# A fused attention and feed-forward kernel: the wide products of the layer stage cut into four products of 32 rows each

## Chip, cores and metric

The kernel runs on one core of a Trainium2 chip. The metric is the device time of one execution in microseconds (us); less is better.

## What is computed

The reference adds eight blocks to x, of 16 sequences x 256 tokens x 128 numbers, one after the other: a cross attention, a stack of six layers, and six further blocks. The change touches only the stack of six layers (`_L0_ffn_ref`). What matters of one layer, with 16 heads of 64 and windows of 32 tokens:

```python
qkv = shift_tokens(x) @ Wqkv              # 128 -> 3 * 1024
q, k = l2norm(q) * qs, l2norm(k) * ksc    # then rotated by position
sim = einsum('bhwie,bhwje->bhwij', q, look(k)) * 8.0      # each window looks at itself and the one before
x = x + einsum('bhwij,bhwje->bhwie', softmax(masked sim), look(v)) @ Wo
hg = layer_norm(shift_tokens(x)) @ W1 + b1                # 128 -> 2 * 341
a, gate = split(hg, 2)
x = x + (a * gelu(gate)) @ W2 + b2                        # 341 -> 128
```

All tensors are float32.

## The kernel before

The layer stage is `shifted_layers` (from L549). It works in 48 passes (`LAST`: 6 layers x 8 passes, p in the code) over 512 tokens, that is 4 tiles (t) of 128 tokens. A tile's heads go in two groups (g) of 8, so a pass has 8 such half tiles. Each engine has its own order of work, written out by hand, and the engines meet through semaphores only. TensorE's order is `body(p)` (L987 to L1140); it works on half tiles of several passes at once, so that other engines have time between two steps of one half tile.

What TensorE does in a pass, by the line of its instruction:

- `project_k` (L860) and `project_q` (L866), 8 times each: one product of the tile's 128 tokens (held in the array, 128 columns) with 512 columns of the weights, into the whole of a PSUM bank.
- `values_a`, `values_b` (L874), 16 times: four products, each with 32 tokens held and 512 columns streamed, each into 32 rows of one bank. The first two stream one slice of `w_vo`, the last two another.
- `scores` (L906) and `mix` (L930), 8 times each: 16 products of 32 held and 128 streamed columns, four for the four blocks of 32 rows and that for four blocks of columns.
- `turn_q` (L890), `turn_k` (L896), `turn_prob` (L917), 8 times each, and `turn_normed` (L952) once: four transposes of 128x128. `turn_x` (L845), twice: two such.
- `fold` (L943), once: one product of 256 columns.
- `gate_proj` (L962) and `up_proj` (L972), 3 times each: one product of 128, 128 and 85 held columns of `w_1` with 512 tokens. `down_proj` (L981), once: for each of 4 tiles three products that add up, 128 held and 128 streamed columns.

Every float32 product appears in the trace as two records, every transpose as one. Below, a group that holds 128 columns or 85 (a transpose, a fold, a product) is called wide, and one whose products hold 32 columns and write 32 rows is called narrow; before the change `values`, `scores` and `mix` are the narrow ones. The order of one steady pass is this, after its last step comes the first of the next pass. Square brackets mark the groups that are narrow before, round ones those that the change edits; 0, 1, 2 is the chunk k of gate and up.

```
turn_q (proj_k) (proj_q) turn_k up2 turn_prob [values_a] [scores] turn_q (proj_k) (proj_q) fold
turn_prob [values_b] [mix] turn_x (proj_k) turn_k [values_a] [mix] [scores] (down) (proj_q) turn_q
[values_b] (proj_k) turn_k turn_prob [values_a] turn_n (proj_q) turn_q [values_b] [scores] turn_k
(proj_k) (gate0) [values_a] [mix] [scores] turn_prob [values_b] turn_q (proj_q) (proj_k) turn_k
turn_prob (gate1) (proj_q) [mix] [values_a] [scores] turn_q turn_prob [values_b] turn_k gate2
(proj_k) (proj_q) [values_a] [scores] [mix] turn_x (proj_k) [mix] turn_q [values_b] (proj_q) turn_k
turn_prob (up0) [values_a] [scores] turn_q (up1) turn_prob [values_b] turn_k [mix] [values_a]
[scores] [mix] [values_b]
```

The other engines take their data from PSUM: ScalarE squares and copies, VectorE rotates, sums and finds the softmax's maxima, GpSimd adds and scales, and SyncE issues the transfers, weights of the next layer among them.

Of the kernel before, what the change touches and what calls it, by code (L numbers as in the profile page):

```python
# [24 lines left out]
DEPTH, WINDOW, HALF = 6, 32, 341  # L25
# [523 lines left out]
def shifted_layers(nc, x_all, ident, ident_bf, dram, kept, following):  # L549
# [17 lines left out]
    with ExitStack() as ctx:  # L567
        def sb(name, shape, dt=F32):
            return ctx.enter_context(nc.sbuf_tensor("f_" + name, shape, dt))
# [3 lines left out]
        def sem(name):  # L573
            used.append(ctx.enter_context(nc.semaphore("f_" + name)))
            return used[-1]

        bank = [ctx.enter_context(nc.psum_tensor(f"f_bank{i}", [128, 512], F32)) for i in range(8)]
        Q, K, V, T, S, P, Y, F = range(8)

        def flat(i):  # L580
            return bank[i][:, :]

        w_qk, w_vo, w_1, w_2, ln_cols, cols, rot, band, rot_dram = (
            kept[n] for n in ("w_qk", "w_vo", "w_1", "w_2", "ln_cols", "cols", "rot", "band", "rot_dram"))
# [20 lines left out]
        f_nt = sb("f_nt", [128, PASS_TOK])  # L605
        gate = sb("gate", [128, 3, PASS_TOK])
# [18 lines left out]
        q_done, k_done, q_squared, k_squared = sem("q_done"), sem("k_done"), sem("q_squared"), sem("k_squared")  # L625
# [10 lines left out]
        f_gate, gate_in, f_gelu, f_up = sem("f_gate"), sem("gate_in"), sem("f_gelu"), sem("f_up")  # L636
# [5 lines left out]
        def count(p, i):  # L642

            return p * CHUNKS + (i + 1 + AHEAD)

        def live(p, t):

            return not isinstance(p, int) or isinstance(p, Steady) or 0 <= p * PASS_TILES + t < LAST * PASS_TILES

        def has(p, back):  # L650

            return not isinstance(p, int) or isinstance(p, Steady) or 0 <= p - back < LAST
# [186 lines left out]
        def _(pe):  # L839
            nc.tensor.matmul(flat(S), ident_bf[:, :], band[:, 0, :], start=True, stop=True).then_inc(s_opened, 1)  # L840

            def turn_x(s, p):
                pe.wait_ge(x_taken[s], p + 1)
                for t in range(2):
                    turned = nc.tensor.transpose(bank[F][:, 128 * t:128 * t + 128], xw[:, s, 128 * t:128 * t + 128], ident[:, :])  # L845
                turned.then_inc(x_turned[s], 1)

            def chunk_x(t):
                t = t % PASS_TILES
                return xs_t[:, t // 2, 128 * (t % 2):128 * (t % 2) + 128]  # L850

            def project_k(p, t, g):
                i = 2 * t + g
                pe.wait_ge(w_qk_in[g], p * 16 + 16)
                if t % 2 == 0 and g == 0:
                    pe.wait_ge(xs_made[t // 2], p * 2 + 2)

                pe.wait_ge(k_squared, count(p, i - 1))
                pe.wait_ge(k_rotated, count(p, i - 1))
                nc.tensor.matmul(flat(K), chunk_x(t), w_qk[:, 1, 512 * g:512 * g + 512], start=True, stop=True).then_inc(k_done, 1)  # L860

            def project_q(p, t, g):
                i = 2 * t + g
                pe.wait_ge(q_squared, count(p, i - 1))
                pe.wait_ge(q_rotated, count(p, i - 1))
                nc.tensor.matmul(flat(Q), chunk_x(t), w_qk[:, 0, 512 * g:512 * g + 512], start=True, stop=True).then_inc(q_done, 1)  # L866

            def values(t, g, j):

# [82 lines left out]
                    turned = nc.tensor.transpose(bank[F][:, 128 * t:128 * t + 128], f_n[:, 128 * t:128 * t + 128], ident[:, :])  # L952
                turned.then_inc(f_turned, 1)

            def gate_proj(p, k):
                at, n = FF[k]
                if k == 0:
                    pe.wait_ge(w_1_in, p * 32 + 32)
                    pe.wait_ge(f_affine, p + 1)
                else:  # L960
                    pe.wait_ge(gate_in, p * 3 + k)
                nc.tensor.matmul(bank[F][0:n, :], w_1[:, HALF + at:HALF + at + n], f_nt[:, :], start=True, stop=True).then_inc(f_gate, 1)  # L962

            def up_proj(p, k):
                at, n = FF[k]
                if k > 0:
                    pe.wait_ge(f_hidden, p * 3 + k)
                elif has(p, -3):
                    pe.wait_ge(xs_made[0], (p + 3) * 2 + 2)
                else:  # L970
                    pe.wait_ge(gate_in, p * 3 + 3)
                nc.tensor.matmul(bank[F][0:n, :], w_1[:, at:at + n], f_nt[:, :], start=True, stop=True).then_inc(f_up, 1)  # L972

            def down_proj(p):
                pe.wait_ge(f_hidden, p * 3 + 3)
                if has(p, -3):
                    pe.wait_ge(xs_made[1], (p + 3) * 2 + 2)
                pe.wait_ge(w_2_in, p * 16 + 16)
                for t in range(PASS_TILES):
                    for k, n in enumerate((128, 128, ONES_ROW + 1)):  # L980
                        done = nc.tensor.matmul(bank[F][:, 128 * t:128 * t + 128], gate[0:n, k, 128 * t:128 * t + 128], w_2[0:n, k, :],  # L981
                                                start=(k == 0), stop=(k == 2))
                done.then_inc(f_done, 1)

            turn_x(0, 0)

            def body(p):  # L987
                if live(p, -1):
                    turn_q(p, -1, 0)
                if live(p, 0):  # L990
                    project_k(p, 0, 0)
                    project_q(p, 0, 0)
                if live(p, -1):
                    turn_k(p, -1, 0)
                if has(p, 3):
                    up_proj(p - 3, 2)
# [4 lines left out]
                    scores(p, -1, 0)  # L1001
                    turn_q(p, -1, 1)
                if live(p, 0):
                    project_k(p, 0, 1)
                    project_q(p, 0, 1)
                if has(p, 0):
                    fold(p)
                if live(p, -2):
# [5 lines left out]
                if has(p, 0):  # L1014
                    pe.wait_ge(fold_made, p + 1)
                    turn_x(1, p)
                if live(p, 1):
                    project_k(p, 1, 0)
                if live(p, -1):
                    turn_k(p, -1, 1)  # L1020
                if live(p, 0):
# [3 lines left out]
                if live(p, -1):  # L1025
                    scores(p, -1, 1)
                if has(p, 3):
                    down_proj(p - 3)
                if live(p, 1):
                    project_q(p, 1, 0)  # L1030
                if live(p, 0):
                    turn_q(p, 0, 0)
                    values_b(p, 0, 0)
                if live(p, 1):
                    project_k(p, 1, 1)
                if live(p, 0):
                    turn_k(p, 0, 0)
                if live(p, -1):
# [3 lines left out]
                if has(p, 2):  # L1042
                    turn_normed(p - 2)
                if live(p, 1):
                    project_q(p, 1, 1)
                if live(p, 0):
                    turn_q(p, 0, 1)
                    values_b(p, 0, 1)
                    scores(p, 0, 0)
                    turn_k(p, 0, 1)  # L1050
                if live(p, 2):
                    project_k(p, 2, 0)
                if has(p, 2):
                    gate_proj(p - 2, 0)
                if live(p, 1):
                    values_a(p, 1, 0)
                if live(p, -1):
# [6 lines left out]
                    values_b(p, 1, 0)  # L1064
                    turn_q(p, 1, 0)
                if live(p, 2):
                    project_q(p, 2, 0)
                    project_k(p, 2, 1)
                if live(p, 1):
                    turn_k(p, 1, 0)  # L1070
                if live(p, 0):
                    turn_prob(p, 0, 0)
                if has(p, 2):
                    gate_proj(p - 2, 1)
                if live(p, 2):
                    project_q(p, 2, 1)
                if live(p, -1):
                    mix(p, -1, 1)
                if live(p, 1):
# [8 lines left out]
                if has(p, 2):  # L1088
                    gate_proj(p - 2, 2)
                if live(p, 3):  # L1090
                    project_k(p, 3, 0)
                    project_q(p, 3, 0)
                if live(p, 2):
                    values_a(p, 2, 0)
                if live(p, 1):
# [3 lines left out]
                if has(p, -1):  # L1099
                    if has(p, 2):  # L1100
                        pe.wait_ge(gate_in, (p - 2) * 3 + 3)
                    else:
                        pe.wait_ge(xs_made[1], p * 2 + 2)
                    turn_x(0, p + 1)
                if live(p, 3):
                    project_k(p, 3, 1)
                if live(p, 0):
                    mix(p, 0, 1)
                if live(p, 2):
                    turn_q(p, 2, 0)  # L1110
                    values_b(p, 2, 0)
                if live(p, 3):
                    project_q(p, 3, 1)
                if live(p, 2):
                    turn_k(p, 2, 0)
                if live(p, 1):
                    turn_prob(p, 1, 0)
                if has(p, 2):
                    up_proj(p - 2, 0)
                if live(p, 2):  # L1120
                    values_a(p, 2, 1)
                    scores(p, 2, 0)
                    turn_q(p, 2, 1)
                if has(p, 2):
                    up_proj(p - 2, 1)
                if live(p, 1):
                    turn_prob(p, 1, 1)
                if live(p, 2):
# [16 lines left out]
            for p in range(LAST + 3):  # L1145
                body(Steady(p) if 3 <= p < LAST else p)
# [2739 lines left out]
```

## Time and profile before

| | |
|---|---|
| median of 3 runs | 4423.32 us (4418.15 to 4425.26) |
| the profiled execution | 4414.45 us, its span 4412.6 us |
| TensorE busy | 3968.6 us, 90% of the span |
| VectorE, ScalarE, GpSimd busy | 81%, 67%, 50% |
| TensorE's granted clock, mean | 0.933 of full speed |

The span runs from the first instruction to the last, and the execution's time has 1.85 us more around it. A busy share is the time in which at least one instruction of the engine ran; the matmuls overlap, so one that is listed with 1.02 us may be followed by the next 0.86 us after its start. The rows below are read by the distance from start to start for that reason.

### The profile page before, as it was taken

To read this page: it belongs to the slowest core of one execution; us is meant where nothing else is said; L and a number is where in the kernel's file an instruction comes from. 1 tells how busy PE (TensorE), PEld (TensorE's weight loads), DVE (VectorE), ACT (ScalarE), POOL (GpSimd) and SP (SyncE) were. 2 spreads that over 40 slices of the span, in tenths; PEclk is the share of its full clock that TensorE was granted. 3 is DMA by queue.
4 is the path that set the end of the run, shared out by engine and by line. 5 is a ranking of instruction groups with operands and counts; after the bars stand their busy time and mean duration, and the time that the engine had idled before them with its cause. 6 is when DMAs were issued, how large, how long until landed. Compare 5 with 4: busy or idle time off the path is not lost. (4 is left out here: it accounts for less than half of the span.)

```text
span 4412.6 us, 117906 instructions
## 1 busy us (share of the span) xinstructions
PE 3968.6 (90%) x43247; PEld 2389.2 (54%) x43247; DVE 3577.9 (81%) x8501; ACT 2960.0 (67%) x5496; POOL 2218.5 (50%) x1398
## 2 busy tenths in 40 slices
PE   8989999999999999999999999999999854737735
PEld 5645555555555555555555555555555533525534
DVE  7878999899998999989999899989999756466341
ACT  3437778778777778778778778778778655636302
POOL 1016666666666666666666666666666400130006
PEclk9999999999999999999999999999999966868558
DMA  3002223323223323233223332232322200000102
GB/s 103 1 2 66 65 66 69 82 65 70 65 64 87 70 63 68 65 84 71 66 63 68 83 71 66 65 91 65 70 66 66 53 1 13 1 0 14 67 8 37
DMA packets 187147, 249.17 MB, mean 56 GB/s; under 512 B 88660, under 2 KB 129110, under 8 KB 186326
## 3 DMA queue, kind: packets, MB, share of 16 engines
q1 hardware_dynamic: 181078, 238.37, 23.0%
q0 software_dynamic: 5632, 4.33, 0.8%
q8 instruction: 352, 5.77, 0.6%
q14 instruction: 85, 0.70, 0.0%
HBM read 39.55 MB, written 14.30 MB: 12 GB/s over the span
## 5 line engine op out<-in xcount | busy, mean ns | idle before, releaser
L1446 POOL TENSOR_TENSOR f_rot_a<-f_rot_a,f_rot_b 128x1024 f32<-128x1024 f32 x384 | 908.3, 2371 | 302.5 <-DVE f_rot_b L1180 197.2
L1454 POOL TENSOR_TENSOR f_rot_a<-f_rot_a,f_norm 128x1024 f32<-128x1024 f32 x384 | 731.3, 1904 | 648.0 <-DVE f_norm L1198 524.6
L874 PE MATMUL f_bank<-f_w_vo,f_xs_t 128*32 128x512 f32 x6144 | 815.8, 603 | 0.2
L1177 DVE TENSOR_TENSOR f_rot_a<-f_bank,f_rot 128x512 f32<-128x512 f32 x768 | 523.3, 682 | 66.8 <-ACT f_squares L1541 32.5
L1550 ACT ACTIVATE f_vo<-f_bank 128x512 f32<-128x512 f32 x768 | 458.7, 597 | 170.9 <-PE f_bank L874 163.2
L1541 ACT ACTIVATE f_squares<-f_bank 128x512 f32<-128x512 f32 x768 | 455.9, 594 | 116.3 <-PE f_bank L860 68.8
L1564 ACT ACTIVATE f_k_t<-f_bank 64x512 f32<-64x512 f32 x768 | 452.7, 589 | 104.0 <-PE f_bank L896 99.5
L1180 DVE TENSOR_TENSOR f_rot_b<-f_bank,f_rot 128x512 f32<-128x512 f32 x768 | 505.9, 674 | 0.0
L1460 POOL TENSOR_TENSOR f_prob<-f_score,f_stat 128x512 f32<-128x512 f32 x384 | 400.5, 1043 | 188.4 <-DVE f_stat L1230 187.8
L1184 DVE TENSOR_REDUCE f_sums<-f_squares 128x16 f32<-128x1024 f32 x384 | 464.6, 1210 | 4.6 <-ACT f_squares L1541 4.6
L906 PEld LDWEIGHTS f_bank<-f_k_t,f_q_t 128*32 128x32 f32 x12288 | 345.3, 110 | 179.5 <-issue 100.2
L930 PEld LDWEIGHTS f_bank<-f_vo_off,f_prob_t 128*32 128x32 f32 x6144 | 330.8, 110 | 167.4 <-issue 150.7
L860 PE MATMUL f_bank<-f_w_qk,f_xs_t 128*128 128x512 f32 x768 | 402.2, 606 | 15.4 <-DMA f_w_qk<-in_Wqk 8.7
L906 PE MATMUL f_bank<-f_k_t,f_q_t 128*32 128x128 f32 x12288 | 406.0, 273 | 1.2 <-ACT f_bank L1570 0.7
L930 PE MATMUL f_bank<-f_vo_off,f_prob_t 128*32 128x128 f32 x6144 | 406.8, 274 | 0.2
L930 PE MATMUL f_bank<-f_vo,f_prob_t 128*32 128x128 f32 x6144 | 406.8, 274 | 0.0
L866 PE MATMUL f_bank<-f_w_qk,f_xs_t 128*128 128x512 f32 x768 | 402.8, 606 | 1.2 <-DVE f_rot_b L1180 1.2
L1555 ACT ACTIVATE f_q_t<-f_bank 128x512 f32<-128x512 f32 x384 | 227.8, 593 | 259.1 <-PE f_bank L890 259.1
L930 PEld LDWEIGHTS f_bank<-f_vo,f_prob_t 128*32 128x32 f32 x6144 | 330.8, 110 | 0.0
L1226 DVE TENSOR_REDUCE f_stat<-f_score 128x8 f32<-128x512 f32 x384 | 260.1, 677 | 76.8 <-ACT f_score L1574 72.1
L896 PEld LDWEIGHTS f_bank<-ident,f_rot_a 128*128 128x128 f32 x1536 | 181.0, 141 | 219.3 <-issue 155.3
L1218 DVE TENSOR_REDUCE f_stat<-f_bank 128x8 f32<-128x512 f32 x384 | 257.9, 672 | 29.0 <-PE f_bank L906 23.6
(459 smaller groups left out, 7380.8 us busy)
## 6 DMA issues: line engine op xcount, KB each, us to landing
f_vo_off<-f_vo SPq DMA_DIRECT2D x1152, 128.0 KB, 2.3
f_vo_off<-f_vo SPq DMA_DIRECT2D x384, 64.0 KB, 2.1
f_vo_dram<-f_vo_pair SPq DMA_DIRECT2D x48, 128.0 KB, 1.8
f_x_shifted<-s_all SPq DMA_DIRECT2D x48, 128.0 KB
f_x_shifted<-s_all SPq DMA_DIRECT2D x48, 127.0 KB
f_w_qk<-in_Wqk SPq DMA_DIRECT2D x10, 512.0 KB, 4.3
f_w_vo<-f_vo_dram SPq DMA_DIRECT2D x10, 512.0 KB, 4.8
e_w<-in_e_W SPq DMA_DIRECT2D x2, 2048.0 KB, 9.9
```

The source lines that it names most:

```text
L866: nc.tensor.matmul(flat(Q), chunk_x(t), w_qk[:, 0, 512 * g:512 * g + 512], start=True, stop=True).then_inc(q_done, 1)
L874: done = nc.tensor.matmul(bank[V][32 * w:32 * w + 32, :], x[:, at:at + 32], w_vo[:, 4 * g:4 * g + 4, w // 2, :], start=True, stop=True)
L906: done = nc.tensor.matmul(bank[S][32 * w:32 * w + 32, 128 * b:128 * b + 128], q_t[:, g, 128 * b + 32 * w:128 * b + 32 * w + 32], k_t[:, :, ...
L930: done = nc.tensor.matmul(bank[Y][32 * w:32 * w + 32, 0:128], prob_t[:, g, 128 * b + 32 * w:128 * b + 32 * w + 32], source[:, g, 2 * (t % ...
L1177: nc.vector.tensor_tensor(rot_a[:, slot, n, :].rearrange("p (h d) -> p h d", h=GROUP), source, c_tab, ALU.mult)
L1180: nc.vector.tensor_tensor(rot_b[:, g, n, :].rearrange("p (h s d) -> p h s d", h=GROUP, s=2), swapped, s_tab, ALU.mult).then_inc((q_rotated ...
L1184: nc.vector.tensor_reduce(sums[:, g, :], squares[:, g, :, :].rearrange("p n (h d) -> p (n h) d", h=GROUP), AX_X, ALU.add).then_inc(lengths, 1)
L1446: nc.gpsimd.tensor_tensor(rot_a[:, slot, :, :], rot_a[:, slot, :, :], rot_b[:, g, :, :], ALU.add).then_inc(rot_summed, 1)
L1454: nc.gpsimd.tensor_tensor(heads, heads, over(norm[:, 16 * g:16 * g + 16], [128, 16, HEAD_DIM]), ALU.mult).then_inc(qk_normed, 1)
L1541: nc.scalar.activation(squares[:, g, n, :], flat((Q, K)[n]), ACT.Square).then_inc((q_squared, k_squared)[n], 1)
L1550: nc.scalar.activation(vo[:, g, 2 * (t % 2) + j, :], flat(V), ACT.Copy).then_inc((va_copied, vb_copied)[j], 1)
L1564: done = nc.scalar.activation(k_t[r:r + 64, n, 4 * g:4 * g + 4, at:at + 128], flat(T)[r:r + 64, :].rearrange("p (b n) -> p b n", b=4), ACT ...
```

## The change

A new helper `multiply` issues a product either whole or, with `rows=True`, as four products of 32 held columns, each into its own 32 rows of the same bank, all with the same streamed operand. Every call of `project_k` and `project_q` in `body(p)` gets `rows=True`, and so do chunks 0 and 1 of `gate_proj` and `up_proj` and the call of `down_proj`. The chunks of 85 columns (`gate_proj(p - 2, 2)` and `up_proj(p - 3, 2)`), the fold and the transposes stay as they are. The order of the steps, the waits and the counts of the semaphores stay the same; the last of the four products signals. No other engine's code is touched.

```diff
+            def multiply(to, left, right, rows):
+
+                size = 32 if rows else left.shape[1]
+                for at in range(0, left.shape[1], size):
+                    part = slice(at, at + size)
+                    done = nc.tensor.matmul(to[part, :], left[:, part], right, start=True, stop=True)
+                return done
...
-            def project_k(p, t, g):
+            def project_k(p, t, g, rows=False):
...
-                nc.tensor.matmul(flat(K), chunk_x(t), w_qk[:, 1, 512 * g:512 * g + 512], start=True, stop=True).then_inc(k_done, 1)
...
+                multiply(flat(K), chunk_x(t), w_qk[:, 1, 512 * g:512 * g + 512], rows).then_inc(k_done, 1)
...
-                nc.tensor.matmul(bank[F][0:n, :], w_1[:, HALF + at:HALF + at + n], f_nt[:, :], start=True, stop=True).then_inc(f_gate, 1)
...
+                multiply(bank[F][0:n, :], w_1[:, HALF + at:HALF + at + n], f_nt[:, :], rows).then_inc(f_gate, 1)
...
                     for k, n in enumerate((128, 128, ONES_ROW + 1)):
-                        done = nc.tensor.matmul(bank[F][:, 128 * t:128 * t + 128], gate[0:n, k, 128 * t:128 * t + 128], w_2[0:n, k, :],
-                                                start=(k == 0), stop=(k == 2))
+                        for at in range(0, 128, 32 if rows else 128):
+                            size = 32 if rows else 128
+                            done = nc.tensor.matmul(bank[F][at:at + size, 128 * t:128 * t + 128], gate[0:n, k, 128 * t + at:128 * t + at + size], w_2[0:n, k, :],
+                                                    start=(k == 0), stop=(k == 2))
...
                 if live(p, 0):
-                    project_k(p, 0, 0)
-                    project_q(p, 0, 0)
+                    project_k(p, 0, 0, rows=True)
+                    project_q(p, 0, 0, rows=True)
...
                 if has(p, 3):
-                    down_proj(p - 3)
...
+                    down_proj(p - 3, rows=True)
```

`project_q` and `up_proj` are edited in the same way as `project_k` and `gate_proj`, and the other calls in `body(p)` as the ones shown.

## Rows read from the trace of the kernel before

**Rows 1.** The page's first part: busy time, share of the span and instructions.

```profile
PE 3968.6 (90%) x43247; PEld 2389.2 (54%) x43247; DVE 3577.9 (81%) x8501; ACT 2960.0 (67%) x5496; POOL 2218.5 (50%) x1398
```

**Rows 2.** Windows: busy us of each engine, granted clock, DMA share, GB/s.

```profile
280.00:320.00 40.00, 27.43 (x108) 18.03 (x109) 24.80 (x62) 10.60 (x20) 10.11 (x6) 0.79 0.01 4
...
1000.00:2000.00 1000.00, 994.88 (x12298) 578.72 (x12291) 914.86 (x1946) 776.18 (x1416) 642.12 (x391) 1.00 0.31 71
```

**Rows 3.** Waits of TensorE from 1000 to 3000 us: total, times, longest.

```profile
PE f_bank L860 <- DMA f_w_qk<-in_Wqk: 7.0, 4, 1.8
PE f_bank L860 <- DVE f_rot_b L1180: 2.1, 3, 0.9
```

**Rows 4.** Groups by line and form, 460 to 3400 us: busy us, mean ns.

```profile
L874 PE MATMUL f_bank<-f_w_vo,f_xs_t 128*32 128x512 f32 x5680 | 753.2, 602 | 0.0
...
L866 PE MATMUL f_bank<-f_w_qk,f_xs_t 128*128 128x512 f32 x710 | 371.1, 604 | 0.3 <-DVE f_rot_b L1180 0.3
```

**Rows 5.** Timeline of TensorE, 2005 to 2014 us: start, us, line, operands, records.

```profile
2005.32 1.04 PE L874 MATMUL f_bank<-f_w_vo,f_xs_t 128*32 128x512 f32 x8
2006.17 1.06 PE L906 MATMUL f_bank<-f_k_t,f_q_t 128*32 128x128 f32 x32
2007.16 0.66 PE L890 MATMUL f_bank<-ident,f_rot_a 128*128 128x128 f32 x4
2007.65 0.60 PE L917 MATMUL f_bank<-ident,f_prob 128*128 128x128 f32 x4
2008.18 1.07 PE L874 MATMUL f_bank<-f_w_vo,f_xs_t 128*32 128x512 f32 x8
2009.18 0.66 PE L896 MATMUL f_bank<-ident,f_rot_a 128*128 128x128 f32 x4
2009.67 1.02 PE L962 MATMUL f_bank<-f_f_nt,f_w 128*85 128x512 f32 x2
2010.53 1.02 PE L860 MATMUL f_bank<-f_w_qk,f_xs_t 128*128 128x512 f32 x2
2011.39 1.02 PE L866 MATMUL f_bank<-f_w_qk,f_xs_t 128*128 128x512 f32 x2
2012.34 1.06 PE L874 MATMUL f_bank<-f_w_vo,f_xs_t 128*32 128x512 f32 x8
2013.22 1.06 PE L906 MATMUL f_bank<-f_k_t,f_q_t 128*32 128x128 f32 x32
2014.10 0.27 PE L930 MATMUL f_bank<-f_vo_off,f_prob_t 128*32 128x128 f32 x1
```

**Rows 6.** The same view at 2001 us: transposes between wide neighbours.

```profile
2001.73 0.60 PE L896 MATMUL f_bank<-ident,f_rot_a 128*128 128x128 f32 x4
2002.17 0.60 PE L917 MATMUL f_bank<-ident,f_prob 128*128 128x128 f32 x4
2002.61 1.02 PE L962 MATMUL f_bank<-f_f_nt,f_w 128*128 128x512 f32 x2
```

**Rows 7.** The same view at 2018 us: a product behind four narrow ones.

```profile
2017.91 1.06 PE L874 MATMUL f_bank<-f_w_vo,f_xs_t 128*32 128x512 f32 x8
2018.91 1.12 PE L866 MATMUL f_bank<-f_w_qk,f_xs_t 128*128 128x512 f32 x2
2019.87 0.60 PE L896 MATMUL f_bank<-ident,f_rot_a 128*128 128x128 f32 x4
```

**Rows 8.** The same view at 2025 us: transposes between narrow neighbours.

```profile
2025.45 1.06 PE L874 MATMUL f_bank<-f_w_vo,f_xs_t 128*32 128x512 f32 x8
2026.45 0.66 PE L896 MATMUL f_bank<-ident,f_rot_a 128*128 128x128 f32 x4
2027.03 0.30 PE L930 MATMUL f_bank<-f_vo_off,f_prob_t 128*32 128x128 f32 x1
```

**Rows 9.** The same view at 2046 us: the down product.

```profile
2046.87 2.94 PE L981 MATMUL f_bank<-f_w,f_gate 128*128 128x128 f32 x24
2049.65 1.02 PE L866 MATMUL f_bank<-f_w_qk,f_xs_t 128*128 128x512 f32 x2
```

More of the change, by code:

```diff
@@ L859, in project_k, with project_q @@
                 pe.wait_ge(k_rotated, count(p, i - 1))
-                nc.tensor.matmul(flat(K), chunk_x(t), w_qk[:, 1, 512 * g:512 * g + 512], start=True, stop=True).then_inc(k_done, 1)
-            def project_q(p, t, g):
+                multiply(flat(K), chunk_x(t), w_qk[:, 1, 512 * g:512 * g + 512], rows).then_inc(k_done, 1)
+            def project_q(p, t, g, rows=False):
                 i = 2 * t + g
@@ L865, in project_q @@
                 pe.wait_ge(q_rotated, count(p, i - 1))
-                nc.tensor.matmul(flat(Q), chunk_x(t), w_qk[:, 0, 512 * g:512 * g + 512], start=True, stop=True).then_inc(q_done, 1)
+                multiply(flat(Q), chunk_x(t), w_qk[:, 0, 512 * g:512 * g + 512], rows).then_inc(q_done, 1)
             def values(t, g, j):
@@ L953, in turn_normed, with gate_proj @@
                 turned.then_inc(f_turned, 1)
-            def gate_proj(p, k):
+            def gate_proj(p, k, rows=False):
                 at, n = FF[k]
@@ L961, in gate_proj, with up_proj @@
                     pe.wait_ge(gate_in, p * 3 + k)
-                nc.tensor.matmul(bank[F][0:n, :], w_1[:, HALF + at:HALF + at + n], f_nt[:, :], start=True, stop=True).then_inc(f_gate, 1)
-            def up_proj(p, k):
+                multiply(bank[F][0:n, :], w_1[:, HALF + at:HALF + at + n], f_nt[:, :], rows).then_inc(f_gate, 1)
+            def up_proj(p, k, rows=False):
                 at, n = FF[k]
@@ L971, in up_proj, with down_proj @@
                     pe.wait_ge(gate_in, p * 3 + 3)
-                nc.tensor.matmul(bank[F][0:n, :], w_1[:, at:at + n], f_nt[:, :], start=True, stop=True).then_inc(f_up, 1)
-            def down_proj(p):
+                multiply(bank[F][0:n, :], w_1[:, at:at + n], f_nt[:, :], rows).then_inc(f_up, 1)
+            def down_proj(p, rows=False):
                 pe.wait_ge(f_hidden, p * 3 + 3)
@@ L1003, in body @@
                 if live(p, 0):
-                    project_k(p, 0, 1)
-                    project_q(p, 0, 1)
+                    project_k(p, 0, 1, rows=True)
+                    project_q(p, 0, 1, rows=True)
                 if has(p, 0):
@@ L1017, in body @@
                 if live(p, 1):
-                    project_k(p, 1, 0)
+                    project_k(p, 1, 0, rows=True)
                 if live(p, -1):
@@ L1027, in body @@
                 if has(p, 3):
-                    down_proj(p - 3)
+                    down_proj(p - 3, rows=True)
                 if live(p, 1):
-                    project_q(p, 1, 0)
+                    project_q(p, 1, 0, rows=True)
                 if live(p, 0):
@@ L1034, in body @@
                 if live(p, 1):
-                    project_k(p, 1, 1)
+                    project_k(p, 1, 1, rows=True)
                 if live(p, 0):
@@ L1044, in body @@
                 if live(p, 1):
-                    project_q(p, 1, 1)
+                    project_q(p, 1, 1, rows=True)
                 if live(p, 0):
@@ L1051, in body @@
                 if live(p, 2):
-                    project_k(p, 2, 0)
+                    project_k(p, 2, 0, rows=True)
                 if has(p, 2):
-                    gate_proj(p - 2, 0)
+                    gate_proj(p - 2, 0, rows=True)
                 if live(p, 1):
@@ L1066, in body @@
                 if live(p, 2):
-                    project_q(p, 2, 0)
-                    project_k(p, 2, 1)
+                    project_q(p, 2, 0, rows=True)
+                    project_k(p, 2, 1, rows=True)
                 if live(p, 1):
@@ L1073, in body @@
                 if has(p, 2):
-                    gate_proj(p - 2, 1)
+                    gate_proj(p - 2, 1, rows=True)
                 if live(p, 2):
-                    project_q(p, 2, 1)
+                    project_q(p, 2, 1, rows=True)
                 if live(p, -1):
@@ L1090, in body @@
                 if live(p, 3):
-                    project_k(p, 3, 0)
-                    project_q(p, 3, 0)
+                    project_k(p, 3, 0, rows=True)
+                    project_q(p, 3, 0, rows=True)
                 if live(p, 2):
@@ L1105, in body @@
                 if live(p, 3):
-                    project_k(p, 3, 1)
+                    project_k(p, 3, 1, rows=True)
                 if live(p, 0):
@@ L1112, in body @@
                 if live(p, 3):
-                    project_q(p, 3, 1)
+                    project_q(p, 3, 1, rows=True)
                 if live(p, 2):
@@ L1118, in body @@
                 if has(p, 2):
-                    up_proj(p - 2, 0)
+                    up_proj(p - 2, 0, rows=True)
                 if live(p, 2):
@@ L1124, in body @@
                 if has(p, 2):
-                    up_proj(p - 2, 1)
+                    up_proj(p - 2, 1, rows=True)
                 if live(p, 1):
```

## Prediction

> **What bounds the kernel now.** I read the page's first part, then the windows, then TensorE's waits, then its timeline. The first part names TensorE as the busiest engine, with 90% of the span [rows 1]. That is a mean over unlike stages, so the windows come next. In the layer stage TensorE is busy 994.88 of 1000 us, VectorE, the next one, 914.86; the granted clock is 1.00, the higher of its two levels [rows 2]. A busy share of 99% can hide waiting, as each matmul is listed until its modelled end, so the waits have to say it too: over 2000 us of this stage TensorE stood 7.0 us for weights of the next layer and 2.1 us for VectorE [rows 3]. The stage is bound by the chain of TensorE's own groups. From 460 to 3400 us there are 710 records of `project_q`, 16 in a pass, which is 44.4 passes of 66.3 us; the 5680 records of `values`, 128 in a pass, give the same count [rows 4].
>
> The last view is the timeline, read from start to start, with the order of the pass beside it. A wide product before a wide group takes 0.86 us (2010.53 to 2011.39), four narrow ones of `values` between narrow groups 0.85 us (2005.32 to 2006.17), and `scores` before a narrow group 0.88 us (2013.22 to 2014.10) [rows 5]. Four transposes between wide groups take 0.44 us (2002.17 to 2002.61) [rows 6]. So a product cut into four of 32 columns takes the same time as the whole one: the four run side by side.
>
> What costs time is the change between wide and narrow. **Entry**, wide to narrow: the transposes before it take 0.53 in place of 0.44, the product before it 0.95 in place of 0.86, and the first narrow group 0.88 in place of 0.85 (2007.65, 2011.39, 2012.34) [rows 5, 6]. I take 0.09 + 0.02 = 0.11 us. **Exit**, narrow to wide: the last narrow group takes 0.99 or 1.00 in place of 0.88 (2006.17, 2008.18), that is 0.12 us, and the first wide group behind it is late as well: transposes take 0.49 in place of 0.44 (2007.16, 2009.18), 0.05 us more [rows 5, 6]; a product takes 0.96 in place of 0.86 (2018.91 to 2019.87), 0.10 us more [rows 7]. The two add up where a group has both: transposes between narrow neighbours take 0.58 (2026.45 to 2027.03), which is 0.44 + 0.05 + 0.09 [rows 8]. The profile thus shows the drain where engine and line stay busy, without a row of idle time.
>
> The Trainium skill (TensorEngine Tiling (Array Packing), Key Properties) says that a change of the tiling mode, not of the tile alone, drains the engine. It gives no price; the trace agrees with it, by the 0.09 and 0.12 us above. It speaks against this change wherever that makes more borders than it removes, and a sum that left the borders out would be the one of the first rival below.
>
> **Does this account for a pass?** By the order of the pass there are 16 entries and 16 exits before; of the exits 13 lead to transposes, 3 to a product (two projections, down). Their price is 16 x 0.11 + 16 x 0.12 + 13 x 0.05 + 3 x 0.10 = 4.63 us. The groups alone: 22 products x 0.86 = 18.9; 25 groups of transposes x 0.44 = 11.0; `turn_x` twice and the fold, estimated at half a group of transposes and half a product, 0.9; `values` 16 x 0.85 = 13.6; `scores` and `mix` 16 x 0.88 = 14.1; down 2.78 (2046.87 to 2049.65) [rows 9] less the 0.10 of its exit, 2.68. Together 61.2 + 4.6 = 65.8 us of the measured 66.3. So this ledger is nearly the whole pass, and at most 0.5 us of it is waiting.
>
> **The change, part by part.** All of it is TensorE's; no transfer, wait or order is moved, and each signal is still given by the last product of a group.
>
> - *The 16 projections and 4 of the gate and up products.* Each becomes four narrow ones on the pattern of `values`: 0.85 to 0.88 in place of 0.86 (20 groups, -0.2 to +0.4 us). I take 0. What no row shows is four parts that all stream the same operand; in `values` two and two do, without a cost [rows 5].
> - *Down.* Each of the 12 products becomes four, as in `mix` and `scores`, whose 16 products take 0.88. So 3 x 0.88 = 2.64 in place of 2.68: -0.04.
> - *Borders that vanish.* Five edited products stood before `values` or `mix` (5 entries: -0.55); three stood behind `values_b` or `scores` (3 exits to a product: 3 x 0.22 = -0.66). Sum -1.21.
> - *Borders that appear.* Eleven entries: ten from transposes or `turn_x` to a projection, gate or up, one from the wide chunk of 85 columns to a projection (11 x 0.11 = +1.21). Nine exits: five projections before `turn_k`, two before `turn_q`, one before the fold, one up product before `turn_prob` (9 x (0.12 + 0.05) = +1.53). The fold behind a narrow group is not in the rows; between 0.05 and 0.10 I take 0.05. Sum +2.74.
>
> So 22 entries and 22 exits stand after: 2.74 - 1.21 - 0.04 = **+1.49 us a pass**. With an uncertainty of 0.02 us on each border (20 new, 8 gone, so up to 0.25 net for the six pairs more) and the bounds of the products it lies between 1.0 and 2.1.
>
> Nothing covers this: TensorE is the chain, and what gets later is each signal behind it, the copies of ScalarE and the rotation of VectorE, which has 85 of 1000 us to spare [rows 2]. There are 48 passes; in the first, while the stage fills, TensorE is busy 27.43 of 40 us at a clock of 0.79 [rows 2], so I count 47. 47 x 1.49 = 70 us. The profiled execution took 4414.45 us (span 4412.6 and 1.85 around it), so it would become 4484; it lies 9 us under the median of the runs, 4423.32. I predict against the median: **4493 us**, 1.6% slower. Its own range is 47 x 1.0 to 47 x 2.1, 4470 to 4522.
>
> **The rivals.**
>
> 1. *Not slower: the price belongs to `values`, `scores` and `mix`, not to the width.* All borders shown have one of these three groups on the narrow side; if their own operands (loads of 32 columns from tiles that other engines have just written) made the delay, the products cut in four would neither pay nor save it. Then only down's 0.04 stays: -2 us, 4421. Against it: `values` (512 columns, held tokens) and `scores` (128 columns, held queries) pay the same 0.12 [rows 5], so operand and size don't matter. It decides where the new borders cost under 1.25 of their 2.74 us. If they were free and the old ones were still saved, the kernel would be 47 x 1.25 = 59 us faster, 4364.
> 2. *Part is absorbed.* Up to 0.5 us of each pass is waiting by the ledger, and a later TensorE waits less. Then 47 x 1.0 = 47 us, 4470. Against it: the waits listed are for weights of the next layer, which come no earlier [rows 3].
> 3. *Four parts with one streamed operand don't run side by side.* If only two could, as the pairs in `values`, 20 groups would take 0.86 us more each: 17.2 us a pass, 808 in all beside the 70, 5300. For it: no row has all four on one operand. Against it: the pairs cost nothing. Of the same kind is a lack of instructions, as 120 records more for the products and 72 for down join some 815 of a pass; but `scores` already runs 32 records in 0.88 us, 27 ns each, and nothing new is denser.
>
> The Trainium skill (TensorE: Matmul & The Clock Gate, Measured speedup vs the span model) gives 2.38 times for three column tiles, so three take 3 / 2.38 = 1.26 times one. By it, as an estimate, 20 groups would cost at least 0.26 x 0.86 more each, 210 us in all, some 4700. The trace so far disagrees, with 0.85 us for four against 0.86 for one, so this milder form of the third rival gets 0.02 of that rival's chance.
>
> **How the numbers follow.** The forecast 0.76; absorbed 0.09; price tied to the three groups 0.06; new borders free 0.04; the third rival 0.05 in both its forms. Something under 0.2% (9 us) can't be told from no change here. Slower: 0.76 + 0.09 + 0.05 = 0.90; same 0.06; faster 0.04. The range takes in the forecast's bounds and the absorbed case, whose low end is 1.0 - 0.4 = 0.6 us a pass, 28 us: 4450 to 4525. It leaves out 0.15.
>
> **What would show it.** Right: in the timeline 1.00 from a projection to `turn_k` or `turn_q`, 0.49 for the transposes behind it (0.58 where the next is narrow), 0.53 for transposes before a projection, 0.86 to 0.88 from one narrow product to the next, 2.64 for down; 67.8 us a pass, with TensorE's listed waits as they were. Wrong: 0.86 from a projection to transposes (rival 1); fewer or shorter waits with all borders paid (rival 2); 1.7 us from a projection to the next group, or idle time without a releaser (rival 3).

## Result and the profile after

The changed kernel takes 4502.84 us (median of 4 runs, 4497.85 to 4505.23), the kernel before in the same comparison 4423.41 us: ratio 1.0178, 95% interval 1.0165 to 1.0192. That is 79.4 us slower; 70 were forecast. The profiled execution's span is 4503.4 us, 90.8 more than before, but 8.2 of that lies behind the last down product, in stages that the change does not touch (856.0 us before, 864.2 after). From the first down product to the last it is 3036.5 us before and 3117.1 after, 80.6 more.

The first part of the page of the changed kernel, to be read against [rows 1]:

```profile
PE 4048.2 (90%) x52460; PEld 2268.4 (50%) x52463; DVE 3583.8 (80%) x8501; ACT 2974.6 (66%) x5496; POOL 2224.6 (49%) x1398
```

TensorE has 9213 records more and 79.6 us more of busy time; its weight loads (PEld) are busy 120.8 us less. The other engines do the same work, and their busy time changes by less than 0.5%. Windows of the layer stage, against [rows 2], with the columns of those rows:

```profile
1000.00:2000.00 1000.00, 992.37 (x14731) 523.49 (x14727) 889.60 (x1890) 760.40 (x1378) 628.28 (x381) 1.00 0.30 69
2000.00:3000.00 1000.00, 997.50 (x14858) 528.37 (x14851) 899.41 (x1903) 761.26 (x1383) 628.62 (x384) 1.00 0.29 67
```

TensorE stays full at the same clock, and VectorE, which was at 914.86 of 1000, now has more time to spare: nearly all of the price lies in TensorE's own time and leaves no idle row. The listed waits of TensorE from 1000 to 3000 us, against [rows 3], show no new one (four borders of layers lie in this window before, three after):

```profile
PE f_bank L847 <- DMA f_w_qk<-in_Wqk: 8.0, 3, 3.0
PE f_bank L847 <- DVE f_rot_b L1190: 2.1, 3, 1.0
```

The groups by line, 460 to 3400 us, against [rows 4]: `values` and the cut projections, which have 128 records a pass each and so 43.2 passes, 68.1 us a pass in place of 66.3.

```profile
L882 PE MATMUL f_bank<-f_w_vo,f_xs_t 128*32 128x512 f32 x5528 | 730.4, 600 | 0.0
L847 PE MATMUL f_bank<-f_w_qk,f_xs_t 128*32 128x512 f32 x5528 | 702.3, 603 | 17.9 <-DMA f_w_qk<-in_Wqk 13.9 <-DVE f_rot_b L1190 4.0
```

The timeline of TensorE in one pass of the changed kernel, against [rows 5 to 9]; the rows of `mix` between 1612.12 and 1612.99 are left out:

```profile
1609.65 1.06 PE L847 MATMUL f_bank<-f_w_qk,f_xs_t 128*32 128x512 f32 x8
1610.65 0.66 PE L904 MATMUL f_bank<-ident,f_rot_a 128*128 128x128 f32 x4
1611.24 1.06 PE L882 MATMUL f_bank<-f_w_vo,f_xs_t 128*32 128x512 f32 x8
...
1612.99 1.06 PE L914 MATMUL f_bank<-f_k_t,f_q_t 128*32 128x128 f32 x32
1613.87 2.82 PE L991 MATMUL f_bank<-f_w,f_gate 128*32 128x128 f32 x96
1616.50 1.04 PE L847 MATMUL f_bank<-f_w_qk,f_xs_t 128*32 128x512 f32 x8
1617.47 0.66 PE L898 MATMUL f_bank<-ident,f_rot_a 128*128 128x128 f32 x4
1618.06 1.06 PE L882 MATMUL f_bank<-f_w_vo,f_xs_t 128*32 128x512 f32 x8
1618.94 1.04 PE L847 MATMUL f_bank<-f_w_qk,f_xs_t 128*32 128x512 f32 x8
1619.92 0.66 PE L904 MATMUL f_bank<-ident,f_rot_a 128*128 128x128 f32 x4
1620.41 0.60 PE L925 MATMUL f_bank<-ident,f_prob 128*128 128x128 f32 x4
```

Read from start to start: a projection before `turn_k` takes 1.00 us (1609.65) where the whole one took 0.86; the transposes behind it, with `values` next, 0.59 (1610.65); down 2.63 (1613.87) in place of 2.78; the projection behind it, narrow before and wide after, 0.97 (1616.50); `scores` before down 0.88 in place of 0.99; `values` before a narrow projection 0.88 (1618.06) in place of 1.00; `turn_k` behind a narrow projection 0.49 (1619.92).

The length of a steady pass comes out of the fold, which runs once in each. The first two rows are of the kernel before, the next two, in a fence of their own, of the changed one:

```profile
1575.48 0.59 PE L943 MATMUL f_bank<-f_wo_pair,f_wv_pair 128*128 128x256 f32 x2
1641.35 0.59 PE L943 MATMUL f_bank<-f_wo_pair,f_wv_pair 128*128 128x256 f32 x2
```

```profile
1538.82 0.70 PE L951 MATMUL f_bank<-f_wo_pair,f_wv_pair 128*128 128x256 f32 x2
1606.35 0.70 PE L951 MATMUL f_bank<-f_wo_pair,f_wv_pair 128*128 128x256 f32 x2
```

65.87 us before, 67.53 after: 1.66 us a pass more, against 1.49 forecast. The two passes around a border of layers are longer, at the second of the five borders 136.32 us before, 4.58 more than two steady ones, and 140.71 after, 5.65 more. All five together exceed steady passes by 19.2 us before (3.0 to 4.6 each) and by 25.9 after (4.3 to 5.9). There TensorE waits for the keys' and queries' weights of the next layer:

```profile
1389.48 0.66 PE L898 MATMUL f_bank<-ident,f_rot_a 128*128 128x128 f32 x4
1393.12 3.55 PE L847 MATMUL f_bank<-f_w_qk,f_xs_t 128*32 128x512 f32 x16 [2.98 <-DMA f_w_qk<-in_Wqk]
1396.60 0.66 PE L904 MATMUL f_bank<-ident,f_rot_a 128*128 128x128 f32 x4
```

After the wait the two projections take 3.48 us (1393.12 to 1396.60) where two narrow ones take 1.85 elsewhere (1565.66 to 1567.51). Over the layer stage this wait was 8.7 us before and is 13.9 after, for five borders.

### The profile page after: what moved, and what is told of

It reads as the page before. It is cut to its first block and busy times, and to the rows that moved or that the text cites. A ratio compares the mean times of both kernels' runs of the same rounds, so it can differ in the third digit from the quotient of the medians.

```text
span 4503.4 us, 136335 instructions
## 1 busy us (share of the span) xinstructions
PE 4048.2 (90%) x52460; PEld 2268.4 (50%) x52463; DVE 3583.8 (80%) x8501; ACT 2974.6 (66%) x5496; POOL 2224.6 (49%) x1398
## 5 line engine op out<-in xcount | busy, mean ns | idle before, releaser
L847 PE MATMUL f_bank<-f_w_qk,f_xs_t 128*32 128x512 f32 x6144 | 781.8, 604 | 22.7 <-DMA f_w_qk<-in_Wqk 13.9
L938 PEld LDWEIGHTS f_bank<-f_vo_off,f_prob_t 128*32 128x32 f32 x6144 | 340.3, 110 | 151.8 <-issue 135.8
L938 PEld LDWEIGHTS f_bank<-f_vo,f_prob_t 128*32 128x32 f32 x6144 | 340.0, 110 | 0.0
L847 PE MATMUL f_bank<-f_f_nt,f_w 128*32 128x512 f32 (+1 forms) x1728 | 308.8, 612 | 17.2 <-DVE f_gate L1277 12.0
L847 PEld LDWEIGHTS f_bank<-f_w_qk,f_xs_t 128*32 128x32 f32 x6144 | 160.1, 109 | 325.0 <-issue 307.7
L904 PEld LDWEIGHTS f_bank<-ident,f_rot_a 128*128 128x128 f32 x1536 | 161.1, 141 | 294.3 <-issue 179.5
```

What stands on the lines that cost most here:

```text
L847: done = nc.tensor.matmul(to[part, :], left[:, part], right, start=True, stop=True)
L938: done = nc.tensor.matmul(bank[Y][32 * w:32 * w + 32, 0:128], prob_t[:, g, 128 * b + 32 * w:128 * b + 32 * w + 32], source[:, g, 2 * (t % ...
```

## Experiments

The kernels are named e1 to e9; ratios are to the kernel before.

**e1: only nine of the 21 calls cut.** The nine are those that move a border or turn an exit to a product into one to transposes:

```diff
-                    project_k(p, 0, 0, rows=True)
-                    project_q(p, 0, 0, rows=True)
+                    project_k(p, 0, 0)
+                    project_q(p, 0, 0)
...
                     project_k(p, 1, 1, rows=True)
```

> Only nine of the 21 calls are cut in four: project_k(1,1), project_q(3,1), down and project_q(1,0), which stand beside a narrow group so that an exit to a product becomes an exit to transposes, and gate 0, project_q(2,1), project_q(3,0), project_k(3,1) and up 0, which stand before a narrow group so that an entry only moves one place. Borders (the forecast's theory): 16 entries and 16 exits as before, 0.20 us a pass less (three exits of 0.17 in place of 0.22, down 0.06 shorter), 48 passes: -10 us, ratio 0.998. Rival, the cut products themselves cost more (the 79 us spread evenly over 21 calls, 0.08 us each): 9 x 0.08 x 48 = +34 us, ratio 1.008.

Measured: 4425.32 us, ratio 1.0006 (0.9996 to 1.0015). Both were wrong: not 34 us slower, so a cut product costs nothing by itself; but the 10 us did not come out. A steady pass is 65.87 us, the same as before to a hundredth. The place of the loss is `project_q(1,1)`; TensorE's timeline in e1:

```profile
1594.55 0.66 PE L960 MATMUL f_bank<-ident,f_f_n 128*128 128x128 f32 x4
1595.17 1.10 PE L847 MATMUL f_bank<-f_w_qk,f_xs_t 128*128 128x512 f32 x2
1596.10 0.60 PE L898 MATMUL f_bank<-ident,f_rot_a 128*128 128x128 f32 x4
```

and VectorE's rotation that this product waits for:

```profile
1594.35 0.68 DVE L1190 TENSOR_TENSOR f_rot_b<-f_bank,f_rot 128x512 f32<-128x512 f32 x1
```

The transposes take 0.62 in place of 0.49, and the product starts 0.14 us after the rotation's end at 1595.03. The rotation begins 14.99 us after the fold of its pass (1579.36); in the kernel before it is 14.97 (1590.45 and 1575.48), with the product 0.18 us behind its end. So TensorE's own time and VectorE's stretch from the fold to this rotation, in which its rows follow without a gap, are equally long in the kernel before; what TensorE saves inside that stretch it waits for.

**e2: only the other twelve calls cut**, those whose neighbours stay wide when the nine are whole. The diff is the opposite of e1's.

> The other twelve of the 21 calls are cut in four, those whose neighbours stay wide when the nine are left whole. Borders: more entries and exits than with all 21, +2.78 us a pass by the ledger, 48 passes: +133 us, ratio 1.030, so half the change costs more than the whole. Rival, each cut product costs the same wherever it stands: 12/21 of 79 us = +45 us, ratio 1.010.

Measured: 4552.7 us, ratio 1.0289 (1.0274 to 1.0305), a steady pass of 68.59 us, 2.72 more than before. Twelve of the 21 calls cost 130 us where all 21 cost 79. A price per cut product cannot give that; a price per border does, and to 2%.

**e3: the changed kernel with the next layer's weights loaded earlier**, on SyncE's queue:

```diff
+                    if q == PASSES - 1 and r == PASS_TILES - 1 and not last:
+                        next_qk(p, layer, 0)
                     if r > 0 or q > 0 or not first:
                         shift_values(p, r - 1, 0)
+                    if q == PASSES - 1 and r == PASS_TILES - 1 and not last:
+                        next_qk(p, layer, 1)
...
```

`next_qk` holds the waits and the load of one half of these weights, which stood behind the shifts.

> The changed kernel with one more edit on SyncE's queue: in the last pass of a layer the loads of the next layer's key and query weights are issued as soon as the last products that read the old ones are done, ahead of the shifts of the values of tile 2, not behind them. Theory: at each of the 5 borders of layers TensorE waits for this transfer and then runs at the lower clock for some products; the two passes around a border are 5.6 us longer than two others after the change, and 4.6 us before it, and both would nearly vanish: 5 x 5 = -25 us against the changed kernel, near 4478, ratio 1.012 to before. Rival: the wait is the transfer's own time, which other transfers stretch, so it stays wherever it is issued: 4503, ratio 1.018.

Measured: 4478.97 us, ratio 1.0122 (1.0107 to 1.0138), 24 us less than the changed kernel. SyncE's queue in e3 at one border of layers:

```profile
1370.98 0.66 SPq L679 DMA_DIRECT2D f_w_qk<-in_Wqk  x1
...
1377.99 0.62 SPq L679 DMA_DIRECT2D f_w_qk<-in_Wqk  x1
```

and TensorE's first products of the next layer in e3:

```profile
1385.42 1.92 PE L852 MATMUL f_bank<-f_w_qk,f_xs_t 128*32 128x512 f32 x16
1387.27 0.66 PE L909 MATMUL f_bank<-ident,f_rot_a 128*128 128x128 f32 x4
```

The loads are issued 14.4 and 7.4 us ahead of these products, which take their usual 1.85 us, and no wait of TensorE for them is listed any more. The two passes around the border are now 136.30 us, 1.3 more than two steady ones; all five borders together exceed steady passes by 4.7 us in place of 25.9.

**e4: two groups moved in the kernel before, nothing cut.**

```diff
                     mix(p, 0, 0)
+                    mix(p, 0, 1)
+                if live(p, 2):
+                    values_b(p, 2, 0)
...
                     turn_x(0, p + 1)
...
-                    mix(p, 0, 1)
...
                     turn_q(p, 2, 0)
-                    values_b(p, 2, 0)
```

> The kernel before, all products whole, with two groups moved in TensorE's order: mix(0,1) and values_b(2,0) directly behind mix(0,0), ahead of turn_x, project_k(3,1) and turn_q(2,0). Nothing is cut. Borders: two entries and two exits fewer a pass, -0.62 us by the ledger, 48 passes: -30 us, 4394, ratio 0.993. Rival, no gain because values_b now waits for ScalarE's copy of values_a, which had more time before: same or up to 0.5 us a pass more, ratio 1.000 to 1.005.

Measured: 4472.63 us, ratio 1.0115 (1.0099 to 1.013): slower by 50 us, more than even the rival said. TensorE's and then ScalarE's timeline in e4:

```profile
1637.09 1.07 PE L882 MATMUL f_bank<-f_w_vo,f_xs_t 128*32 128x512 f32 x8 [0.75 <-ACT f_vo L1560]
```

```profile
1633.60 1.28 ACT L1610 ACT_TABLE_LOAD   x1
1634.89 1.67 ACT L1610 ACTIVATE f_gate<-f_gate 128x512 f32<-128x512 f32 x3
1636.47 0.57 ACT L1560 ACTIVATE f_vo<-f_bank 128x512 f32<-128x512 f32 x1
```

`values_b` needs ScalarE's copy of `values_a`, and that stands behind a load of the function table and three GELUs. The rival was right in kind and too small in size: two borders saved, 0.97 us a pass lost.

**e5: e1 with `turn_q(0,1)` moved ahead of `project_q(1,1)`.**

```diff
+                if live(p, 0):
+                    turn_q(p, 0, 1)
                 if live(p, 1):
                     project_q(p, 1, 1)
                 if live(p, 0):
-                    turn_q(p, 0, 1)
                     values_b(p, 0, 1)
```

> The kernel with nine calls cut (e1), with turn_q(0,1) moved ahead of project_q(1,1) in TensorE's order. In e1 the steady pass is 65.87 us as before, though the borders are 0.21 us fewer; the transposes ahead of project_q(1,1) take 0.62 in place of 0.49 and the product 0.93 in place of 0.86, and VectorE's rotation that project_q(1,1) waits for ends at a fixed distance behind the fold. Theory: the saving is lost in that wait; with half a us of other work ahead of the product it comes out: 65.66 us a pass, -10 us against the kernel before, ratio 0.998. Rival: the next wait takes its place, or the saving was never there: 65.87, ratio 1.000 to 1.001.

Measured: 4417.97 us, ratio 0.9991 (0.9982 to 1.0). A steady pass is 65.67 us, as the theory said to a hundredth, so the wait for VectorE was what took e1's saving. Of the 10 us 4.5 reach the end, and the interval reaches 1.000, so by the time alone that is not told apart from no change. In the profiled execution the five borders of layers take back about as much as the passes save: they exceed steady passes by 28.0 us, against 19.2 before, and the listed waits for the weights there are 12.5 us in the whole stage, against 8.7.

**e6: of e4's two moves only `mix(0,1)`.** The diff is e4's without the lines of `values_b`.

> The kernel before, nothing cut, with mix(0,1) alone moved directly behind mix(0,0), ahead of turn_x and project_k(3,1); values_b(2,0) stays where it was. One entry and one exit fewer, -0.29 us a pass by the ledger. In e4 the loss sat behind the two mixes, where values_b waited for ScalarE. Theory: without that move the border comes out in full, as the wait of e1 lies in another part of the pass: 65.58 us a pass, -14 us, ratio 0.997. Rival: every saving of TensorE is eaten by a wait, since the other engines' chain takes 65.87 us as well: ratio 1.000.

Measured: 4419.98 us, ratio 0.9995 (0.9986 to 1.0004), a steady pass of 65.86 us. The rival holds. The 0.29 us saved at the mixes are lost at `up_proj` 0, which takes 1.11 us in place of 0.96, and at the `values` and `scores` behind it, 0.99 and 1.01 in place of 0.88 and 0.99.

**e8: the kernel before with e3's early loads alone.**

> The kernel before with the early loads alone. Theory: the two passes around a border of layers lose nearly all of the 4.6 us by which they exceed two others: 5 x 4.3 = -21 us, 4402, ratio 0.995. Rival: only in the changed kernel, which is later there, does the early load help: ratio 1.000.

Measured: 4410.63 us, ratio 0.9967 (0.9954 to 0.9981). The two passes around the second border are 0.67 us longer than two steady ones in place of 4.58, so the theory holds there. By the ratio 15 of the 21 us come out. The trace shows where the others are: all five borders together exceed steady passes by 4.2 us in place of 19.2, which is these 15 us; the forecast had taken the second border, the longest before, for all five.

**e7: e6's move, e5's move, early loads, and eight of e1's nine cuts** (without `project_k(3,1)`).

> Together: the nine cut calls less project_k(3,1), mix(0,1) behind mix(0,0), turn_q(0,1) ahead of project_q(1,1), and the early loads of the next layer's weights. If all comes out: -0.50 us a pass (24 us) and 4.6 us at each of 5 borders of layers (23 us): 4376, ratio 0.989. If the passes keep their 65.87 us and only the loads help: 4400, ratio 0.995.

Measured: 4398.89 us, ratio 0.9948 (0.9935 to 0.9962), steady passes of 65.67 us: the loads and e5's saving come out, the border of the mixes does not.

**e9: e7 with `project_k(3,1)` cut and put directly behind the mixes**, ahead of `turn_x`.

> As e7, with project_k(3,1) cut in four as well and put directly behind the two mixes, ahead of turn_x. In e6 the 0.29 us of the border were lost at up 0, which waits for ScalarE's shifted copy of what turn_x made: up 0 takes 1.11 in place of 0.96 and the values behind it 0.99 in place of 0.88. ScalarE squares the keys of project_k(3,1) ahead of that copy. Theory: with the product earlier the copy is earlier too, the wait goes and the border comes out: 65.38 us a pass in place of 65.67 in e7, 14 us less than e7, 4385, ratio 0.992. Rival: another wait takes its place, so 65.6 to 65.7 us a pass, 4399, ratio 0.995.

Measured: 4395.15 us, ratio 0.9943 (0.993 to 0.9957), steady passes of 65.68 us: the rival again. It is the fastest kernel of the study, 24 us under the kernel before, and not told apart from e7. ScalarE's timeline in e9 shows why another order at this place gives nothing:

```profile
1606.15 1.28 ACT L1615 ACT_TABLE_LOAD   x1
1607.45 1.67 ACT L1615 ACTIVATE f_gate<-f_gate 128x512 f32<-128x512 f32 x3
1609.03 0.58 ACT L1565 ACTIVATE f_vo<-f_bank 128x512 f32<-128x512 f32 x1
1609.62 1.28 ACT L1589 ACT_TABLE_LOAD   x1
...
1613.69 0.60 ACT L1565 ACTIVATE f_vo<-f_bank 128x512 f32<-128x512 f32 x1
1614.18 1.18 ACT L1579 ACTIVATE f_k_t<-f_bank 64x512 f32<-64x512 f32 x2
```

and TensorE's weight loads of the `values` and `scores` behind `up_proj` 0 wait for what comes out of it:

```profile
1614.40 0.19 PEld L887 LDWEIGHTS f_bank<-f_w_vo,f_xs_t 128*32 128x32 f32 x8 [0.87 <-issue]
1615.41 0.81 PEld L919 LDWEIGHTS f_bank<-f_k_t,f_q_t 128*32 128x32 f32 x32 [0.83 <-ACT f_k_t L1579]
```

The load for `values` starts 0.11 us after the copy that empties its bank (1614.29), the load for `scores` 0.05 us after the copy of the keys (1615.36); in e6 and e7 the distances are the same, 0.11 to 0.12 and 0.05. (For `values` the profile names no releaser; that it waits for this copy stands in its code.) So the forecast had the wrong wait: `up_proj` 0 itself starts 0.53 us behind the transposes, as elsewhere, and looks long from start to start because the `values` behind it are held. From 1606.15 on ScalarE runs without a gap up to these copies, two table loads of 1.28 us among it. That this stretch is the bound of the pass there is read from the rows; no run shortened it.

## Why the prediction was right

*TensorE is the chain.* Right for every loss: the borders that appear cost in full, in the changed kernel (1.66 us a pass, nearly all of it borders) and in e2 (2.72, ledger 2.78). For a gain it was only half of it, as e1, e6 and e9 show: at two places of the pass, VectorE's and ScalarE's stretches are as long as TensorE's. The prediction took VectorE's 85 of 1000 us for room; they are, but not in every stretch of a pass. With a forecast of slower this did not matter.

*Four products side by side for the price of one.* Right, also with one streamed operand for all four. The changed kernel's `gate_proj` 0, which stands between a narrow projection and `values`, takes 0.86 us:

```profile
1559.91 1.04 PE L847 MATMUL f_bank<-f_f_nt,f_w 128*32 128x512 f32 x8
1560.77 1.04 PE L882 MATMUL f_bank<-f_w_vo,f_xs_t 128*32 128x512 f32 x8
```

That settles the third rival in both its forms; the milder one, 1.26 times one product, would be 1.08 us.

*The price of a border.* Right to a hundredth where a row of before existed: 1.00, 0.59, 0.49, 0.97, 0.88. The fold behind a narrow product takes 0.53 to 0.54 in place of 0.43, so 0.10, the upper end of the bounds, where 0.05 was taken. What in TensorE makes up the price, no run separates. In the rows under the sum below, the weight loads of the group at an entry start only with the group itself (1586.62 both), and those between two narrow groups 0.05 us ahead (1587.46 for 1587.51).

*Eleven entries more, five fewer, nine exits more, three fewer.* Right, and e1 and e2 show that it is their place and not the number of cuts that counts. The first rival, that the price belongs to `values`, `scores` and `mix`, falls with e2.

*Down.* 2.63 in place of 2.64 forecast.

*The sum.* 1.49 us a pass became 1.66. Of the 0.17, the fold is 0.05, and entries at 0.115 in place of 0.11 give 0.03 for six more. Most of the rest is a wait that the ledger did not have, behind `up_proj` 0 in the changed kernel:

```profile
1586.62 1.06 PE L847 MATMUL f_bank<-f_f_nt,f_w 128*32 128x512 f32 x8
1587.51 1.05 PE L882 MATMUL f_bank<-f_w_vo,f_xs_t 128*32 128x512 f32 x8
```

```profile
1586.62 0.16 PEld L847 LDWEIGHTS f_bank<-f_f_nt,f_w 128*32 128x32 f32 x8 [0.17 <-issue]
1587.46 0.19 PEld L882 LDWEIGHTS f_bank<-f_w_vo,f_xs_t 128*32 128x32 f32 x8 [0.68 <-issue]
1588.48 0.81 PEld L914 LDWEIGHTS f_bank<-f_k_t,f_q_t 128*32 128x32 f32 x32 [0.83 <-ACT f_k_t L1574]
```

`values` takes 0.97 us there (1587.51 to 1588.48) in place of the 0.86 between narrow groups, as `scores` behind it waits for ScalarE's copy of the keys, which ends at 1588.42; it is the copy that e9 waits for too. That is 0.11 us a pass, and 0.02 more at `scores`; against it, `project_q(1,1)` no longer waits the 0.04 us that it did before (0.90 us, 1591.31 to 1592.21, in place of 0.86).

How the passes add up is read from the starts of the 48 folds, of which the first and the last lie 80.1 us further apart than before. Each of the 44 distances from the fourth on has the 1.66 us, 73 us in all; the first three, while the stage fills, have nothing (193.10 us before, 193.14 after); the borders of layers add 6.7. The forecast, 47 x 1.49 = 70, counted three passes too many, which made up for 4.5 of the 7.5 us that its price was short. That it lies so near is in part luck.

*The second rival, absorption.* Its premise, up to 0.5 us of waiting in each pass, came from the mean pass of 66.3 us, which has the borders of layers in it; a steady pass is 65.87 us against 65.8 in the ledger, so there was next to nothing to absorb. And it was wrong in sign: the waiting for the weights at the borders of layers did not shrink, it grew by 5.2 us. The prediction said that these weights come no earlier; it did not see that they come later against TensorE. The four issues of SyncE ahead of these loads took 3.77 us at the border shown (1385.29 to 1389.06) where they took 2.41 before (1360.98 to 1363.39). At each of the five borders of the changed kernel one of the four is long, 1.08 to 1.95 us, and at none before; the wait is 2.12 us behind the one of 1.08 and 2.77 to 3.15 behind the others, in place of 1.68 to 1.81. e3 shows that the load's place behind them makes the wait; why one issue is long there is open.

## What to carry to other kernels

Cutting a product into four of 32 columns neither gained nor cost by itself here; what counts is the sequence of widths on TensorE. Count the changes of width in the order of work, price each from start-to-start distances in the timeline (here 0.11 us in, 0.17 to 0.22 out), and cut only where a product stands next to narrow work. In a kernel whose engines are tuned to each other an added border can cost in full, while one removed may bring nothing until the waits of the other engines are moved as well.

## What was not expected of the hardware

The wait for one transfer at a border of layers can cost more than its own length. Windows of the changed kernel around the second border, columns as in [rows 2]:

```profile
1390.00:1393.00 3.00, 0.14 (x2) 0.00 (x0) 1.55 (x4) 1.22 (x3) 2.56 (x4) 1.00 0.57 194
1393.00:1397.00 4.00, 3.88 (x20) 0.98 (x21) 0.35 (x1) 0.85 (x2) 1.08 (x1) 0.57 0.88 282
```

TensorE stood 2.98 us, and the granted clock of the next 4 us was 0.57, so for most of them at the lower of its two levels, 1.2 GHz; the two projections took 1.63 us longer than elsewhere. Not every such wait is followed by this. The windows behind the waits at three other borders of the changed kernel, then at two of the kernel before:

```profile
847.40:850.70 3.30, 3.30 (x17) 0.62 (x17) 0.00 (x0) 0.60 (x1) 0.79 (x1) 0.56 0.98 309
2484.40:2489.00 4.60, 4.54 (x22) 1.81 (x23) 0.48 (x1) 2.22 (x4) 1.88 (x2) 0.63 0.71 243
3029.70:3033.20 3.50, 3.46 (x25) 1.46 (x26) 0.13 (x1) 2.07 (x4) 1.22 (x1) 1.00 0.94 295
```

```profile
836.50:839.80 3.30, 3.26 (x12) 1.69 (x13) 0.00 (x0) 1.84 (x4) 2.19 (x2) 1.00 0.88 236
1367.50:1370.90 3.40, 3.35 (x5) 1.27 (x6) 0.00 (x0) 0.60 (x1) 2.27 (x3) 0.56 0.85 283
```

After the change the clock is low behind four of the five waits. Behind that of 2.77 us at the last border it stays at 1.00, and the two projections take 1.85 us, though the DMA engines are as busy there (0.94) as at the others. So the slow products go with the clock and not with the transfers. Before the change the clock is low behind two of the five waits, of 1.72 and 1.75 us, and at 1.00 behind those of 1.68, 1.79 and 1.81. The length of the wait alone does not decide it, and no run shows what does. In the changed kernel the waits are 13.9 us and the slow products some 6.4 more, 20 us together; in e3, which has no such wait at any of the five borders, they exceed steady passes by 21.2 us less.
